# Gate layer of a graph network: TensorE gathers three of sixteen tiles, GpSimd thirteen

## The chip, the cores and the metric

The kernel runs on one core of one Trainium2 chip. The metric is the device time of one execution in microseconds (us); shorter is better. The engines are TensorE (PE, with its weight loads PEld), VectorE (DVE), ScalarE (ACT), GpSimd (POOL) and SyncE (SP). They run side by side and wait for one another through semaphores.

## The reference, cut to what matters

Four graph layers run over 3,125 nodes with 96 features and 100,000 edges sorted by target node: a power iteration, three graph convolutions, a message layer and a gate layer. Each gets `relu(layernorm(x))` and is added to `x`. The change is in the gate layer (two small loads for it lie in the message layer):

```python
edge_input = concatenate([x[src], edge_attr], axis=-1)        # 96 + 32 features
messages = gelu(edge_input @ mW1 + mb1) @ mW2 + mb2
gates = sigmoid(gelu(edge_input @ gW1 + gb1) @ gW2 + gb2)
aggregated = segment_sum(messages * gates, dst)
combined = concatenate([x, aggregated], axis=-1)
h = x + gelu(combined @ uW1 + ub1) @ uW2 + ub2                # then a layernorm
```

## The kernel before, in words

The edges are cut into 784 tiles of 128 and these into 98 groups of 8 (`GT`). Two groups, an even and an odd one, make a pair. Each tile needs its 128 source nodes' values, and there are two ways to get them.

*By GpSimd.* At the end of the message layer the product of every node with both first weights (192 values) is written to a table in memory. For six tiles of each group (`BY`) GpSimd issues an indirect DMA that fetches 128 rows of that table into `rows`, a ring of seven groups (L1322). TensorE multiplies the tiles' edge features with the edge part of the weights (`mix_edges`, L1539): three tiles at a time lie in three blocks of 32 partitions, two halves make six products. VectorE adds the six products to the six gathered tiles with one instruction (`add_edges`, L1437).

*By TensorE.* For the other two tiles of each group (`ON`), thus four a pair or 512 edges, SyncE loads the source numbers to 125 partitions (`load_row`), ScalarE turns them into 16-bit numbers (`widen`, L1343), and VectorE compares them with each of 25 blocks of 125 node numbers (`make_picks`, L1412): 25 instructions a pair of 512 columns, 13 in one group and 12 in the next. TensorE multiplies these selection matrices with the nodes' features in two 16-bit parts (`collect`, L1549): 50 matmuls a pair into a PSUM bank, two banks taking turns. ScalarE copies the result to `inputs` (L1350), and TensorE applies bias and weights (`mix_inputs`, L1559 and L1562).

Then, for all eight tiles: ScalarE takes the gelu of both (`activate`, L1357 to L1365), into `gated` and into `passed`, which has six slots; VectorE forms the gate sum (`sum_gates`, L1443, L1446); ScalarE takes a tanh (L1371); VectorE makes one-hot target matrices (`make_onehots`, L1471, L1473, and the addition of earlier sums, L1454); TensorE sums the messages (`sum_messages`, L1573).

The order is written out by hand in turns. In turn t VectorE does the addition of group t, the gate sum of t-1, the one-hots of t-2 and half of the picks of a later pair:

```python
for turn in range(NG + 2):
    if turn < NG:
        add_edges(turn)
    if 0 < turn <= NG:
        sum_gates(turn - 1)
    if turn > 1:
        steps = make_onehots(turn - 2)
    if (turn + 4) // 2 < NG // 2:
        make_picks((turn + 4) // 2, turn % 2)
```

TensorE's turn is the edge products of the next group (these wait for VectorE's addition, as they share the banks), half a collection, the input products of the next group, and the message sums of t-2. GpSimd runs ahead until the ring of seven is full, then it waits for ScalarE's last read of a slot (`rows_used`). After its last gather it does two wide sums of 125 x 2400 elements (L1327, L1329), for the end of the layer.

Of the kernel before, what the change touches and what calls it, by code (L numbers as in the profile page):

```python
# [6 lines left out]
D = 96  # L7
# [17 lines left out]
EPS = 1e-5  # L25
LOADS = 23
FAR = 8192.0
# [5 lines left out]
EDGES = 4  # L33
ON = 2
BY = GT - ON
CUT = 13
ROW_LIFT = 4096.0
MIDDLE = 1600.0
KEPT = 6
SLOTS = 3  # L40
# [761 lines left out]


def tiles_picked(groups):

    return groups // 2 * PICKED + groups % 2 * 2


class GateInputs:


    def __init__(self, nc, ctx, weights):
# [11 lines left out]
        self.t = space[0:NP, 6272:6272 + NT * D].rearrange("p (t d) -> p t d", d=D)  # L824
        self.gate_pick = space[0:NP, 8704:8704 + NT * ON * EP].bitcast(F16).rearrange("p (t e) -> p t e", t=NT)
        self.parts = m.sb("parts", [NP, NT, 2 * D], F16)
# [3 lines left out]
        self.wh = m.sb("wh", [D, 2 * D], F32)  # L830
        self.we = m.sb("we", [3 * DE, 2 * D], F32)
        self.b1 = m.sb("b1", [NP, 2 * D], F32)
# [24 lines left out]
def message_layer(nc, g, src_rows, dst, edges, w1, b1, w2, b2, pre):  # L857

    with ExitStack() as ctx:
# [40 lines left out]
        def _(sp):  # L900
# [12 lines left out]
            for group in range(NG):  # L913
# [307 lines left out]
def gated_layer(nc, g, pre, edges_T, on_edges_T, on_src, out):  # L1221
# [4 lines left out]
    with ExitStack() as ctx:  # L1226
# [13 lines left out]
        src_row = m.sb("src_row", [NP, 2, 2 * ON * EP], I32)  # L1240
        src_near = m.sb("src_near", [NP, 2, 2 * ON * EP], F16)
        ones = m.sb("ones", [128, 128], BF16)
        bias = m.sb("bias", [128, ON, 2 * D], BF16)
        bias_part = m.sb("bias_part", [NP, 2, 2 * D], BF16)
# [30 lines left out]
        def _(sp):  # L1275
# [3 lines left out]
            def load_row(c):  # L1279
                if c >= 2:  # L1280
                    sp.wait_ge(widened, c - 1)
                sp.dma_start(src_row[:, c % 2, :], on_src[c, :].unsqueeze(0).to_broadcast([NP, 2 * ON * EP])
                             ).then_inc(row_loaded[c % 2], 16)
# [26 lines left out]
        def _(pool):  # L1310
# [22 lines left out]
        def _(act):  # L1333
# [12 lines left out]
            def collect(c):  # L1346
                act.wait_ge(gathered, 2 * (c + 1))
                if c >= 2:
                    act.wait_ge(on_mixed, 2 * (c - 1))
                nc.scalar.activation(inputs[0:D, c % 2, :], collected[c % 2], ACT.Copy).then_inc(collected_out, 1)  # L1350

            def activate(group):
                r = rows[:, group % RING, :, :]
# [3 lines left out]
                nc.scalar.activation(gated[:, group % 2, BY:GT, :], product[:, :, D:2 * D], ACT.Gelu  # L1357
                                     ).then_inc(gate_in, 1)
                if group >= KEPT:
                    act.wait_ge(group_done, group - KEPT + LAG + 1)  # L1360
                nc.scalar.activation(passed[:, group % KEPT, BY:GT, 0:D], product[:, :, 0:D], ACT.Gelu
                                     ).then_inc(on_used, 1)
                act.wait_ge(added, group + 1)
                nc.scalar.activation(gated[:, group % 2, 0:BY, :], r[:, :, D:2 * D], ACT.Gelu).then_inc(gate_in, 1)
                nc.scalar.activation(passed[:, group % KEPT, 0:BY, 0:D], r[:, :, 0:D], ACT.Gelu  # L1365
                                     ).then_inc(rows_used, 1)
# [31 lines left out]
        def _(dve):  # L1398
# [25 lines left out]
            link(nc.vector.tensor_tensor(bias_rest[:, 1, :], bias_rest[:, 0, :], bias_part[:, 1, :], ALU.subtract))  # L1424
            for k in range(ON):
                link(nc.vector.tensor_copy(bias[0:1, k, :], b1[0:1, :]))
# [97 lines left out]
        def _(pe):  # L1524
# [7 lines left out]
            def mix_edges(group):  # L1532
                pe.wait_ge(edge_ready[group % SLOTS], 16 * (group // SLOTS + 1))
                if group:
                    pe.wait_ge(added, group)
                for half in range(2):
                    for k in range(3):
                        at = slice(DE * k, DE * (k + 1))
# [4 lines left out]
            def collect(c, part):  # L1543
                pe.wait_ge(picked, NT * c + (CUT, NT)[part])
                if c >= 2:
                    pe.wait_ge(collected_out, c - 1)
                for j in range(*((0, CUT), (CUT, NT))[part]):
                    for i in range(2):
                        last = nc.tensor.matmul(collected[c % 2], parts[:, j, i * D:(i + 1) * D], pick[:, j, :],  # L1549
                                                start=(j == 0 and i == 0), stop=(j == NT - 1 and i == 1))  # L1550
                last.then_inc(gathered, 1)

            def mix_inputs(group):
# [3 lines left out]
                if group:  # L1557
                    pe.wait_ge(on_used, group)
                nc.tensor.matmul(product, ones[:, :], bias[:, :, :], start=True, stop=False)  # L1559
                for i in range(ON):  # L1560
                    at = (group % 2 * ON + i) * EP
                    last = nc.tensor.matmul(product[:, i, :], inputs[:, c % 2, at:at + EP], w1[:, :],  # L1562
                                            start=False, stop=(i == ON - 1))
                last.then_inc(on_mixed, 1)
# [136 lines left out]
```

## Time and profile before

| | us |
|---|---|
| median of three runs | 3346.31 (3342.11 to 3347.23) |
| the profiled execution | 3346.54 |
| its span | 3344.5 |
| granted TensorE clock over the span | 0.948 |
| busy: PE / DVE / POOL / ACT | 2896.9 / 2424.0 / 1144.0 / 780.9 |

The gate layer takes about the last 970 us of the span. The numbers are of one profiled execution. In a line of a group, "x" is the count; then come busy time in us and the mean of one in ns, and the idle time of its engine just before, with what ended it. In a timeline a row is start, length, engine, line, operation, output<-input, shapes and count; instructions of one kind that follow each other are merged. Records of neighbouring VectorE instructions overlap by some 0.08 us. In a row of busy times by stretch come the stretch, its length, then PE, PEld, DVE, ACT and POOL with their counts, the granted TensorE clock, the share of the DMA engines and GB/s.

### The profile page before, as it was taken

How to read it: one execution, taken by the hardware profiler on the slowest of the kernel's cores; microseconds unless marked ns; L12 is line 12 of the kernel's file. 1: busy time of each engine (PE TensorE's matmuls, PEld its weight loads, DVE VectorE, ACT ScalarE, POOL GpSimd, SP SyncE). 2: the span in 40 equal slices, each digit the busy share in tenths (PEclk: the TensorE clock that was granted, in tenths of full speed). 3: DMA queues.
4: the chain of work that ended last, by engine and by line, in shares of the span. 5: the costliest groups of instructions: out<-in, count | busy, mean ns of one | idle time of the engine just before them, and what ended most of it. 6: DMA issues, size and time to landing. Idle time of an engine off the chain costs nothing. (4 is left out here: it accounts for less than half of the span.)

```text
span 3344.5 us, 73809 instructions
## 1 busy us (share of the span) xinstructions
PE 2896.9 (87%) x25677; PEld 2247.1 (67%) x25678; DVE 2424.0 (72%) x6174; ACT 780.9 (23%) x1414; POOL 1144.0 (34%) x1156
## 2 busy tenths in 40 slices
PE   3677777899999988899799999998699999999985
PEld 0211211699999987777799999997466666666654
DVE  6988777743333364335888888886699999999996
ACT  0133455610000014110211111111133333333321
POOL 0000000000000000000777777774477666666650
PEclk9999989889999998999899999998699999999997
DMA  0000000000000000000544454441344333333320
GB/s 29 0 0 0 0 0 0 2 2 2 2 2 2 2 2 4 1 1 13 134 122 113 117 119 120 118 116 40 90 106 104 98 94 96 98 94 96 98 63 15
DMA packets 102571, 176.68 MB, mean 53 GB/s; under 512 B 35467, under 2 KB 57408, under 8 KB 102284
## 3 DMA queue, kind: packets, MB, share of 16 engines
q0 software_dynamic: 45472, 84.37, 11.1%
q1 hardware_dynamic: 56811, 88.29, 9.3%
q8 instruction: 204, 3.34, 0.4%
q14 instruction: 84, 0.68, 0.1%
HBM read 167.77 MB, written 4.80 MB: 52 GB/s over the span
## 5 line engine op out<-in xcount | busy, mean ns | idle before, releaser
L1322 POOL DMA_INDIRECT gate_rows<-first_rows,all_src_i x588 | 586.2, 997 | 264.3 <-issue 157.3
L951 POOL DMA_INDIRECT msg_rows<-h_rows,all_src_i x539 | 535.7, 994 | 164.2 <-issue 163.8
L1147 PE MATMUL msg_sums<-pre_parts,pre_space 125*128 125x192 f16 x6125 | 528.6, 248 | 37.3 <-DVE pre_space L1025 37.2
L1549 PE MATMUL gate_sums<-pre_space,pre_parts 125*96 125x512 f16 x2450 | 552.3, 382 | 7.0 <-DVE pre_parts L1418 7.0
L938 POOL MEMSET pre_middle<- 125x1 f32 x1 | 0.1, 99 | 1590.6 <-POOLq L649 1590.6
L1147 PEld LDWEIGHTS msg_sums<-pre_parts,pre_space 125*128 125x128 f16 x6125 | 510.3, 99 | 44.0 <-DVE pre_space L1025 39.1
L579 PE MATMUL hop_sums<-dense_work,dense_counts 125*128 125x192 f16 x6250 | 520.6, 247 | 14.2 <-DVE dense_t L533 6.6
L579 PEld LDWEIGHTS hop_sums<-dense_work,dense_counts 125*128 125x128 f16 x6250 | 518.1, 98 | 16.6 <-DVE dense_t L533 7.2
L1549 PEld LDWEIGHTS gate_sums<-pre_space,pre_parts 125*96 125x96 f16 x2450 | 295.1, 124 | 241.0 <-issue 33.0
L422 PE MATMUL cnt_sums<-cnt_hot,cnt_near 128*128 x1000 | 346.2, 407 | 120.2 <-DVE cnt_hot L361 115.0
L1025 DVE TENSOR_SCALAR pre_space<-msg_src_near,pre_node_no 125x640 f16<-125x640 f16 x1225 | 393.7, 394 | 12.0 <-ACT msg_src_near L963 11.8
L1412 DVE TENSOR_SCALAR pre_space<-gate_src_near,pre_node_no 125x512 f16<-125x512 f16 x1225 | 375.1, 379 | 15.4 <-PE gate_sums L1549 8.3
L422 PEld LDWEIGHTS cnt_sums<-cnt_hot,cnt_near 128*128 x1000 | 97.3, 97 | 363.0 <-issue 360.2
L533 DVE TENSOR_REDUCE dense_t<-hop_sums 125x384 f32<-125x768 f32 (+1 forms) x63 | 54.9, 871 | 291.5 <-PE hop_sums L579 291.5
L359 DVE TENSOR_TENSOR cnt_near<-dense_work,cnt_src_n 128x256 f16 x500 | 180.1, 360 | 111.6 <-issue 87.2
L785 PE MATMUL conv_sums<-dense_work,dense_counts 125*128 125x288 bf16 x1875 | 235.7, 290 | 7.9 <-DVE dense_t L714 7.9
L239 ACT ACTIVATE dense_work<-cnt_key,cnt_start_at 128x786 f32<-128x786 f32 x158 | 150.2, 951 | 387.2 <-PE cnt_sums L422 341.0
L785 PEld LDWEIGHTS conv_sums<-dense_work,dense_counts 125*128 125x128 f16 x1875 | 185.8, 99 | 57.6 <-DVE dense_t L714 8.6
L979 ACT ACTIVATE msg_rows<-msg_rows 128x768 f32<-128x768 f32 x98 | 82.7, 844 | 580.5 <-DVE msg_rows L1052 580.5
L367 DVE TENSOR_SCALAR cnt_hot<-dense_work 128x500 f16 x500 | 173.8, 348 | 0.0
L361 DVE TENSOR_SCALAR cnt_hot<-dense_work 128x500 f16 x500 | 172.2, 344 | 0.0
L1573 PE MATMUL gate_sums<-gate_onehot,gate_passed 128*97 128x64 f32 x1584 | 155.9, 254 | 15.4 <-DVE gate_onehot L1473 15.4
(261 smaller groups left out, 3268.4 us busy)
## 6 DMA issues: line engine op xcount, KB each, us to landing
msg_edge<-edges SPq DMA_DIRECT2D x98, 384.0 KB
msg_src_row<-src_rows SPq DMA_DIRECT2D x49, 312.5 KB
gate_src_row<-on_src SPq DMA_DIRECT2D x49, 250.0 KB
gate_edge<-edges SPq DMA_DIRECT2D x98, 96.0 KB
gate_rows<-first_rows,all_src_i POOLq DMA_INDIRECT x588
msg_rows<-h_rows,all_src_i POOLq DMA_INDIRECT x539
gate_inputs<-on_edges SPq DMA_DIRECT2D x49, 64.0 KB, 1.8
first_rows<-pre_space SPq DMA_DIRECT2D x6, 375.0 KB
```

The lines of the kernel that those rows point to most:

```text
L359: nc.vector.tensor_tensor(nears.rearrange("p (c i) -> p c i", i=2), pairs2, low, ALU.is_equal)
L361: nc.vector.tensor_scalar(hots[0], iota, codes[:, 0:ET][:, bass.ds(now, 1)], None, ALU.is_equal).then_inc(ready[0], 1)
L367: nc.vector.tensor_scalar(hots[1], iota, code, None, ALU.is_equal).then_inc(ready[1], 1)
L422: end_of_pair = nc.tensor.matmul(sums[:, b, 0:WIN * NT], nears.rearrange("p (c i) -> p i c", i=2)[:, i, :], hots[i], start=False, stop=Tru ...
L579: last = nc.tensor.matmul(sums[:, g0 + i, 0:2 * D], counts[0:NP, at:at + 128], half[frm][:, k, :], start=(k == 0), stop=(k == NT - 1))
L785: last = nc.tensor.matmul(sums[:, 4 * (q % 2) + i, 0:3 * D], counts[0:NP, at:at + 128], parts[:, j, :], start=(j == 0), stop=(j == NT - 1))
L951: nc.gpsimd.indirect_dma_start(out=rows[:, r, k, :], out_offset=None, in_=table, in_offset=bass.IndirectOffsetOnAxis(ap=src_i[:, at:at + 1 ...
L1025: nc.vector.tensor_scalar(pick[:, c % 2, j, :], src_near[:, c % 2, :], node_no[:, j:j + 1], 1.0 / ROW_LIFT, ALU.is_equal, ALU.mult).then_i ...
L1147: last = nc.tensor.matmul(got[group % 2][:, n, 0:2 * D], pick[:, c % 2, j, i * EP:(i + 1) * EP], parts[:, j, :], start=(j == 0), stop=(j = ...
L1322: nc.gpsimd.indirect_dma_start(out=rows[:, r, k, :], out_offset=None, in_=table, in_offset=bass.IndirectOffsetOnAxis(ap=src_i[:, at:at + 1 ...
L1412: nc.vector.tensor_scalar(pick[:, j, :], src_near[:, c % 2, :], node_no[:, j:j + 1], 1.0 / ROW_LIFT, ALU.is_equal, ALU.mult).then_inc(pick ...
L1549: last = nc.tensor.matmul(collected[c % 2], parts[:, j, i * D:(i + 1) * D], pick[:, j, :], start=(j == 0 and i == 0), stop=(j == NT - 1 an ...
```

## The change

TensorE gathers one tile of each even group and two of each odd one (`ON = (1, 2)`), so 384 edges a pair (`PAIR`) for 512; GpSimd gathers seven and six. The picks, the collected values, the source numbers and the inputs shrink to 384 columns. The seventh tile's edge features lie in a fourth block of 32 partitions, in a half of four tiles; `we` gets a fourth copy of the weights (two more loads in the message layer, `LOADS`). The fourth block's products take PSUM bank 3, so the sums move to 4 and 5, and the collection has bank 6 alone instead of two in turn: TensorE waits for ScalarE's copy before it collects anew. The addition becomes two instructions, one for each half. `passed` has five slots for six.

```diff
-ON = 2
-BY = GT - ON
+ON = (1, 2)
+PAIR = sum(ON) * EP
-KEPT = 6
+KEPT = 5
+def by_dma(group):
+    return GT - ON[group % 2]
...
-        rows = m.sb("rows", [EP, RING, BY, 2 * D], F32)
+        rows = m.sb("rows", [EP, RING, GT - 1, 2 * D], F32)
-        edge = m.sb("edge", [3 * DE, SLOTS, 2, EP], F32)
-        inputs = m.sb("inputs", [D + DE, 2, 2 * ON * EP], F32)
+        edge = m.sb("edge", [4 * DE, SLOTS, 2, EP], F32)
+        inputs = m.sb("inputs", [D + DE, 2, PAIR], F32)
-        total = [sums[0:D + 1, b, 0:SPAN] for b in (3, 4)]
-        collected = [sums[0:D, b, :] for b in (5, 6)]
-        product = sums[:, 7, 0:ON * 2 * D].rearrange("p (k d) -> p k d", k=ON)
+        total = [sums[0:D + 1, b, 0:SPAN] for b in (4, 5)]
+        collected = sums[0:D, 6, 0:PAIR]
+        product = [sums[:, 7, 0:n * 2 * D].rearrange("p (k d) -> p k d", k=n) for n in ON]
...
-                for k in range(BY):
+                for k in range(by_dma(group)):
                     at = group * GT + k
                     nc.gpsimd.indirect_dma_start(
...
             def add_edges(group):
-                turn, r = divmod(group, RING)
-                dve.wait_ge(rows_ready[r], 16 * BY * (turn + 1))
+                r, n = group % RING, by_dma(group)
+                dve.wait_ge(rows_ready[r], 16 * sum(by_dma(i) for i in range(r, group + 1, RING)))
                 dve.wait_ge(edge_mixed, group + 1)
-                to = rows[:, r, :, :].rearrange("p (h k) d -> p h k d", h=2)
-                products = sums[:, 0:3, 0:4 * D].rearrange("p k (h d) -> p h k d", h=2)
-                nc.vector.tensor_tensor(to, to, products, ALU.add).then_inc(added, 1)
+                for half, k0, k1 in ((0, 0, n - 3), (1, n - 3, n)):
+                    to = rows[:, r, k0:k1, :]
+                    products = sums[:, 0:k1 - k0, 2 * D * half:2 * D * (half + 1)]
+                    nc.vector.tensor_tensor(to, to, products, ALU.add).then_inc(added, 1)
...
             def mix_edges(group):
                 pe.wait_ge(edge_ready[group % SLOTS], 16 * (group // SLOTS + 1))
                 if group:
-                    pe.wait_ge(added, group)
-                for half in range(2):
-                    for k in range(3):
+                    pe.wait_ge(added, 2 * group)
+                for half, n in enumerate((by_dma(group) - 3, 3)):
+                    for k in range(n):
...
             def collect(c, part):
                 pe.wait_ge(picked, NT * c + (CUT, NT)[part])
-                if c >= 2:
-                    pe.wait_ge(collected_out, c - 1)
+                if c:
+                    pe.wait_ge(collected_out, c)
...
-                nc.tensor.matmul(product, ones[:, :], bias[:, :, :], start=True, stop=False)
-                for i in range(ON):
-                    at = (group % 2 * ON + i) * EP
+                n, to = ON[group % 2], product[group % 2]
+                nc.tensor.matmul(to, ones[:, :], bias[:, 0:n, :], start=True, stop=False)
+                for i in range(n):
+                    at = (group % 2 * ON[0] + i) * EP
```

## Rows read from the trace of the kernel before

**Rows 1.** Busy time by engine, steady part of the gate layer (first: window length).

```profile
2605.00:3214.00 609.00, 583.14 (x3946) 402.38 (x3946) 572.65 (x1260) 188.37 (x408) 406.95 (x408) 1.00 0.37 96
```

**Rows 2.** Waits in the layer: who waited for whom, us in total, times, longest.

```profile
POOL gate_rows L1322 <- ACT gate_passed L1365: 102.5, 71, 1.7
PE gate_sums L1539 <- DVE gate_rows L1437: 35.5, 44, 1.6
DVE gate_rows L1437 <- PE gate_sums L1539: 2.4, 1, 2.4
```

**Rows 3.** Timeline, VectorE's additions: start us, us, engine line, operation.

```profile
2423.93 1.34 DVE L1437 TENSOR_TENSOR gate_rows<-gate_rows,gate_sums 128x1152 f32<-128x1152 f32 x1
...
2506.03 1.33 DVE L1437 TENSOR_TENSOR gate_rows<-gate_rows,gate_sums 128x1152 f32<-128x1152 f32 x1
...
2524.22 1.33 DVE L1437 TENSOR_TENSOR gate_rows<-gate_rows,gate_sums 128x1152 f32<-128x1152 f32 x1
...
3214.52 1.34 DVE L1437 TENSOR_TENSOR gate_rows<-gate_rows,gate_sums 128x1152 f32<-128x1152 f32 x1
```

**Rows 4.** Timeline, VectorE's picks in stretches, two beside gathers, one without.

```profile
2511.26 3.71 DVE L1412 TENSOR_SCALAR pre_space<-gate_src_near,pre_node_no 125x512 f16<-125x512 f16 x12
...
2520.13 4.17 DVE L1412 TENSOR_SCALAR pre_space<-gate_src_near,pre_node_no 125x512 f16<-125x512 f16 x13
...
3239.26 3.23 DVE L1412 TENSOR_SCALAR pre_space<-gate_src_near,pre_node_no 125x512 f16<-125x512 f16 x12
```

**Rows 5.** Timeline, single gathers and picks, message layer first.

```profile
2165.72 0.95 POOL L951 DMA_INDIRECT msg_rows<-h_rows,all_src_i  x1 [0.30 <-issue]
2166.06 0.37 DVE L1025 TENSOR_SCALAR pre_space<-msg_src_near,pre_node_no 125x640 f16<-125x640 f16 x1
2166.36 0.45 DVE L1025 TENSOR_SCALAR pre_space<-msg_src_near,pre_node_no 125x640 f16<-125x640 f16 x1
...
2511.87 0.95 POOL L1322 DMA_INDIRECT gate_rows<-first_rows,all_src_i  x1 [0.30 <-issue]
2512.12 0.34 DVE L1412 TENSOR_SCALAR pre_space<-gate_src_near,pre_node_no 125x512 f16<-125x512 f16 x1
2512.38 0.55 DVE L1412 TENSOR_SCALAR pre_space<-gate_src_near,pre_node_no 125x512 f16<-125x512 f16 x1
```

**Rows 6.** Groups by line, VectorE: count, busy us, mean ns, idle before.

```profile
L1045 DVE TENSOR_TENSOR msg_rows<-msg_sums,msg_edge 128x192 f32<-128x192 f32 x49 | 16.7, 341 | 2.5 <-PE msg_sums L1147 2.5
```

**Rows 7.** GpSimd: first gather (timeline), gathers of 2424 to 2587.6 by line.

```profile
2378.91 0.95 POOL L1322 DMA_INDIRECT gate_rows<-first_rows,all_src_i  x1 [4.51 <-DMA first_rows<-pre_space]
...
L1322 POOL DMA_INDIRECT gate_rows<-first_rows,all_src_i x127 | 126.2, 994 | 38.7 <-issue 38.7
```

**Rows 8.** Timeline, TensorE's collections and ScalarE's copy of one.

```profile
2167.39 6.35 PE L1147 MATMUL msg_sums<-pre_parts,pre_space 125*128 125x192 f16 x75
...
2392.20 13.87 PE L1549 MATMUL gate_sums<-pre_space,pre_parts 125*96 125x512 f16 x50 [6.97 <-DVE pre_parts L1418]
...
2720.83 0.59 ACT L1350 ACTIVATE gate_inputs<-gate_sums 96x512 f32<-96x512 f32 x1 [4.26 <-PE gate_sums L1549]
...
2724.57 5.81 PE L1549 MATMUL gate_sums<-pre_space,pre_parts 125*96 125x512 f16 x26
```

**Rows 9.** Busy time by engine, part of the counting stage (columns as before).

```profile
500.00:700.00 200.00, 161.72 (x2124) 98.86 (x2124) 152.31 (x446) 110.24 (x192) 0.00 (x0) 0.84 0.00 1
```

**Rows 10.** Timeline, the first 25 picks of message layer and gate layer.

```profile
1603.53 7.97 DVE L1025 TENSOR_SCALAR pre_space<-msg_src_near,pre_node_no 125x640 f16<-125x640 f16 x25 [2.22 <-ACT msg_src_near L963]
...
2381.66 7.87 DVE L1412 TENSOR_SCALAR pre_space<-gate_src_near,pre_node_no 125x512 f16<-125x512 f16 x25 [7.03 <-ACT gate_src_near L1343]
```

**Rows 11.** Timeline around GpSimd's wide sums, and VectorE's last addition.

```profile
3224.95 5.28 POOL L1327 TENSOR_TENSOR pre_space<-all_h,pre_ub 125x2400 f32<-125x2400 f32 x1
3224.97 11.29 DVE L1443 TENSOR_TENSOR pre_space<-pre_space,pre_gw 128x768 f32<-128x768 f32 x1
...
3277.56 1.35 DVE L1437 TENSOR_TENSOR gate_rows<-gate_rows,gate_sums 128x1152 f32<-128x1152 f32 x1
```

More of the change, by code:

```diff
@@ L25 @@
 EPS = 1e-5
-LOADS = 23
+LOADS = 25
 FAR = 8192.0
@@ L925, in _ @@
                         sp.dma_start(to, frm).then_inc(pre.loaded, 16)
-                    for k in range(3):
+                    for k in range(4):
                         sp.dma_start(pre.we[DE * k:DE * (k + 1), 0:D],
@@ L1349, in collect @@
                     act.wait_ge(on_mixed, 2 * (c - 1))
-                nc.scalar.activation(inputs[0:D, c % 2, :], collected[c % 2], ACT.Copy).then_inc(collected_out, 1)
+                nc.scalar.activation(inputs[0:D, c % 2, :], collected, ACT.Copy).then_inc(collected_out, 1)
             def activate(group):
-                r = rows[:, group % RING, :, :]
+                n, values = by_dma(group), product[group % 2]
+                r = rows[:, group % RING, 0:n, :]
                 act.wait_ge(on_mixed, group + 1)
@@ L1356, in activate @@
                     act.wait_ge(gate_sum, group - 1)
-                nc.scalar.activation(gated[:, group % 2, BY:GT, :], product[:, :, D:2 * D], ACT.Gelu
+                nc.scalar.activation(gated[:, group % 2, n:GT, :], values[:, :, D:2 * D], ACT.Gelu
                                      ).then_inc(gate_in, 1)
@@ L1424, in _ @@
             link(nc.vector.tensor_tensor(bias_rest[:, 1, :], bias_rest[:, 0, :], bias_part[:, 1, :], ALU.subtract))
-            for k in range(ON):
+            for k in range(2):
                 link(nc.vector.tensor_copy(bias[0:1, k, :], b1[0:1, :]))
@@ L1534, in mix_edges @@
                 if group:
-                    pe.wait_ge(added, group)
-                for half in range(2):
-                    for k in range(3):
+                    pe.wait_ge(added, 2 * group)
+                for half, n in enumerate((by_dma(group) - 3, 3)):
+                    for k in range(n):
                         at = slice(DE * k, DE * (k + 1))
@@ L1544, in collect @@
                 pe.wait_ge(picked, NT * c + (CUT, NT)[part])
-                if c >= 2:
-                    pe.wait_ge(collected_out, c - 1)
+                if c:
+                    pe.wait_ge(collected_out, c)
                 for j in range(*((0, CUT), (CUT, NT))[part]):
                     for i in range(2):
-                        last = nc.tensor.matmul(collected[c % 2], parts[:, j, i * D:(i + 1) * D], pick[:, j, :],
+                        last = nc.tensor.matmul(collected, parts[:, j, i * D:(i + 1) * D], pick[:, j, :],
                                                 start=(j == 0 and i == 0), stop=(j == NT - 1 and i == 1))
@@ L1558, in mix_inputs @@
                     pe.wait_ge(on_used, group)
-                nc.tensor.matmul(product, ones[:, :], bias[:, :, :], start=True, stop=False)
-                for i in range(ON):
-                    at = (group % 2 * ON + i) * EP
-                    last = nc.tensor.matmul(product[:, i, :], inputs[:, c % 2, at:at + EP], w1[:, :],
-                                            start=False, stop=(i == ON - 1))
+                n, to = ON[group % 2], product[group % 2]
+                nc.tensor.matmul(to, ones[:, :], bias[:, 0:n, :], start=True, stop=False)
+                for i in range(n):
+                    at = (group % 2 * ON[0] + i) * EP
+                    last = nc.tensor.matmul(to[:, i, :], inputs[:, c % 2, at:at + EP], w1[:, :],
+                                            start=False, stop=(i == n - 1))
                 last.then_inc(on_mixed, 1)
@@ L1669 @@
     src, dst = padded(inputs["src"], 0), padded(inputs["dst"], N)
+    blocks = [[[0, 1, 2, 3], [4, 5, 6, 7]], [[0, 1, 2, 6], [3, 4, 5, 7]]]
     edges_32 = padded(inputs["edge_attr_32"], 0).reshape(NG, GT, EP, DE)
@@ L1676 @@
                                    axis=1).reshape(NG // 2, PICKED * EP),
-        "on_src": src.reshape(NG, GT, EP)[:, BY:].reshape(NG // 2, 2 * ON * EP),
+        "on_src": np.concatenate([src.reshape(NG, GT, EP)[i::2, GT - ON[i]:] for i in range(2)],
+                                 axis=1).reshape(NG // 2, PAIR),
         "dst": np.ascontiguousarray(dst.reshape(ET, EP).T),
@@ L1682 @@
                                          .transpose(0, 2, 1, 3)).reshape(NG, EP, GT * D),
-        "edges_32": np.ascontiguousarray(edges_32[:, 0:BY].reshape(NG, 2, 3, EP, DE)
-                                         .transpose(0, 2, 4, 1, 3)).reshape(NG, 3 * DE, 2 * EP),
-        "on_edges_32": np.ascontiguousarray(edges_32[:, BY:].reshape(NG // 2, 2, ON, EP, DE)
-                                            .transpose(0, 4, 1, 2, 3)).reshape(NG // 2, DE, 2 * ON * EP),
+        "edges_32": np.ascontiguousarray(np.stack([edges_32[i::2, blocks[i]] for i in range(2)], axis=1)
+                                         .transpose(0, 1, 3, 5, 2, 4)).reshape(NG, 4 * DE, 2 * EP),
+        "on_edges_32": np.ascontiguousarray(np.concatenate([edges_32[i::2, GT - ON[i]:] for i in range(2)], axis=1)
+                                            .transpose(0, 3, 1, 2)).reshape(NG // 2, DE, PAIR),
     }
```

20 lines of the change are left out of this document (10 added, 10 removed).

## Prediction

> **What bounds the kernel now.** I read the page first: the profiled execution took 3346.54 us, of which its span is 3344.5, against a median of 3346.31, so a difference worked out in the span is taken off 3346.5 as it stands. Then the busy table of the steady part of the gate layer: in 609 us VectorE is busy for 572.65 and TensorE for 583.14, GpSimd for 406.95, ScalarE for 188.37 [rows 1]. Two engines at 94 to 96% could each be the bound, so the list of waits decides. TensorE waits 44 times, 35.5 us in all, for VectorE's addition of the edge products; GpSimd waits 102.5 us for ScalarE to free a row slot; and VectorE waits for that same product of TensorE once in 98 groups, 2.4 us [rows 2]. VectorE is the bound. The reader is to see that TensorE's high share is not the limit, and that GpSimd is ahead.
>
> The yardstick is the start of VectorE's addition L1437: two groups (a pair) take 2524.22 - 2506.03 = 18.19 us while GpSimd still runs freely, and the 44 pairs from 2423.93 to 3214.52 take 790.6 us, 17.97 each on average, since once the ring of seven slots is full GpSimd pauses [rows 3].
>
> VectorE's largest item is the picks L1412, 25 a pair. Where no gather runs, twelve take 3.23 us; beside gathers twelve take 3.71 and thirteen 4.17 [rows 4]. As the record of one pick overlaps the next by about 0.08, the undisturbed step is (3.23 - 0.34) / 11 = 0.263 us. The single picks show where the rest goes: the one that starts 0.25 us after a gather's start takes 0.34, the next, at +0.51, takes 0.55. In the message layer the pick at +0.34 is undisturbed (0.37) and the one at +0.64 takes 0.45 [rows 5]. So near its end a gather holds a pick up. Where it lets go is 2512.38 + 0.55 - 0.08 - 2511.87 = 0.98 us after the gather's start. Gathers come every 1.25 us. Today's picks start at 0.98, 1.24, 0.25 and 0.51 of this cycle and the fourth is held: four picks per gather.
>
> **The change, part by part.** *Picks.* Their width falls from 512 to 384. From 640 to 512 columns the undisturbed pick goes from 0.37 to 0.34 [rows 5], so 128 columns are worth 0.03 by the two digits of these rows; I take 0.033, which lies within their rounding, and the step becomes 0.230. But the time beside gathers is set by the cycle. Starting at 0.98, picks of 0.230 start at 1.21, then 0.19, 0.42 and 0.65 of the next cycle; the last would end at 0.88 and is held to 0.98. That is five per gather, with 0.10 lost where 0.21 was. Today's stretches by the same rule: the first pick (0.64 after the gather of 2510.62) is held for 0.34, then twelve picks take 0.34 + 2 x 1.25 + 3 x 0.263 = 3.63 and thirteen 0.34 + 3 x 1.25 = 4.09, which are the 3.71 and 4.17 of [rows 4] less the overlap. After: 0.34 + 2 x 1.25 + 0.23 = 3.07 and 3.30. A pair of stretches falls from 7.72 to 6.37: -1.35 us. Bounds: nothing gained beside gathers (first rival), or no holding at all, 25 x 0.230 = 5.75. I take 6.37, which only extends what reproduces today's two stretches.
>
> The Trainium skill (page "SBUF — State Buffer", section "Who interferes with whom") says that VectorE in such a mode and GpSimd take one pair of ports, and that whoever issues first has it for the whole instruction while the other is blocked. The trace agrees that they exclude each other but not with the length: if a gather held the pair for its 0.95 us, 25 picks would need 5.75 + 5 x 0.95 = 10.5 us, and 7.7 are measured. Its clause on who issues first is the third rival below.
>
> *Addition of edge products.* One instruction of 1152 elements becomes two: 768 + 576 in even groups, 576 + 576 in odd ones. From 192 elements in 341 ns [rows 6] and 1152 in 1337 the slope is 1.04 ns per element: 0.94 us for 768 and 0.74 for 576, as steps 0.86 and 0.66 against 1.26 now. A pair goes from 2.52 to 1.52 + 1.32 = 2.84: +0.32 us. This is on the path in full.
>
> *GpSimd.* Thirteen gathers a pair for twelve. In the free stretch 127 gathers take 126.2 + 38.7 = 164.9 us, 1.298 each [rows 7]: 13 make 16.88 us.
>
> *VectorE's pair* becomes 18.19 + 0.32 - 1.35 = 17.16 us, 0.28 above GpSimd's 16.88. GpSimd starts some 29 us ahead (its gathers begin at 2378.91 [rows 7], so those of group 2 at about 2378.9 + 15.7 = 2394.6, and VectorE adds to group 2 at 2423.93), stays ahead and hardly pauses. So the relief that VectorE has today from GpSimd's pauses (18.19 against 17.97 on average) goes, which is why I count from 18.19. Over 44 pairs: 44 x (17.97 - 17.16) = -35.6 us.
>
> *TensorE.* A collecting matmul of 512 columns has a step of 5.81 / 26 = 0.223 us, one of 192 columns 6.35 / 75 = 0.085 [rows 8]; by their slope 384 columns take 0.168. 50 a pair give -2.8 us, and even groups lose one input product. Of 17.97 us a pair it is busy today for 583.14 / 609 = 96%, 17.2; that becomes some 14, with over 3 us idle: worth nothing on the path. The seventh tile in the fourth row block adds two of fourteen records to 0.93 us of small matmuls, and even as two serial ones (0.3) it lies in that idle time. If TensorE idles more its clock may dip: in the counting stage, busy 161.72 of 200 us, the granted clock was 0.84 against 1.00 here [rows 1, 9]. At 0.84 its 14 us a pair would be 16.7: still hidden.
>
> *One collecting bank for two.* The next collection waits for ScalarE's copy. The copy starts at 2720.83 and takes 0.59; the next collection starts at 2724.57 [rows 8]. 3.1 us of cover, made of input products, message sums and edge products, which stay. Zero; if the cover went it would cost up to 0.6 on TensorE, not on VectorE.
>
> *SyncE.* Edge blocks grow to 128 partitions, the index rows and inputs shrink by a quarter; they are asked for groups ahead. Two more small loads lie in the message layer. Five instead of six slots of `passed`: the one that is wanted is freed a turn before ScalarE writes it. Zero each.
>
> *Opening,* 2381.66 to 2423.93. Here TensorE's first collection (13.87 us for 50, at a low clock at first) [rows 8] and the first picks (7.87) [rows 10] are in series: -2.7 or so and -1.5, and the first pairs' picks and collections -1.8: together -6.
>
> *Tail,* from 3214.52 to 3277.56, 63.0 us. After the last gather GpSimd's two wide sums run 10.5 us, and L1443 on VectorE takes 11.29 instead of 0.94 [rows 11]. The sums now start at about 2378.9 + 49 x 16.88 + 2 = 3208, when VectorE is near group 95: the 10.3 us are paid as before. After: 2 pairs of 17.16, 3 turns without picks of 5.4, and 10.3: 60.8. -2.2 us.
>
> Sum: -35.6 - 6 - 2.2 = -43.8. 3346.5 - 43.8 = 3302.7, say 3302.5 us.
>
> **Rivals.** *First, slower: still four picks per gather.* For it: 25 picks of 640 columns took 7.97 us beside gathers and 25 of 512 took 7.87 [rows 10]: narrowing brought next to nothing once, since both are four per 1.25. It decides at one point: the pick that starts 0.42 after the gather's start and ends at 0.65. If it is held, the picks gain nothing, the addition's 0.32 stays, and a pair takes 18.51. Against: the message layer's pick from 0.34 to 0.64 is not held [rows 5], practically the same stretch. Price: 44 x 0.54 = +23.8, opening -4, tail +1: 3367 us. Chance 0.12.
>
> *Second, only the columns.* The holds cost what they cost today in total (their phase shifts, and one gather more per pair makes up for a shorter hold), and the picks give 25 x 0.033 = 0.83. A pair 17.68: 44 x 0.29 = -12.8, opening -5, tail -1: 3328 us. For it: holds depend on phases which I only know for today's lengths. Chance 0.20.
>
> *Third, gathers wait for picks, and GpSimd becomes the bound.* Five gathers a pair would each wait up to one pick, 0.23: 16.88 + 1.15 = 18.03, 49 pairs from 2378.9 end at 3262. The last addition then comes at about 3265 instead of 3277.6, but GpSimd's wide sums hold VectorE for 10.3 after it: 3344 us, no change. The skill's clause that issue order decides who blocks would do this. Against: gathers beside picks last 0.95 like others [rows 5]. Chance 0.07.
>
> *Fourth, no holding at all:* VectorE 16.54, so GpSimd's 16.88 is the bound: 44 x 1.09 = -48 and -8: 3290 us. Chance 0.06. My forecast: 0.55.
>
> **Numbers.** 0.2% of 3346 us, 6.7 us, is about what a measurement of this kernel can tell from no change. The range runs from the fourth case to a little beyond the second, 3289 to 3335, and leaves out the first and third (0.19). Faster: forecast, second and fourth, and a little of the third: 0.83; the same 0.05; slower 0.12.
>
> **What would show it.** Right: L1412's successor with 384 columns, twelve in about 3.1 us and thirteen in 3.4 beside gathers; two additions a group; additions 17.1 to 17.2 us apart per pair; few GpSimd waits for ScalarE; TensorE at some 80%. Wrong: most gathers with only four picks between two holds, additions over 18 us apart per pair, gathers of 1.1 us or more beside picks, or VectorE waiting for gathered rows.

## The result, and the profile after

The changed kernel takes 3302.35 us (median of four runs, 3298.76 to 3305.37) against 3346.14 before: ratio 0.9871, 95% interval 0.9859 to 0.9883, so 43.8 us or 1.3% faster. The profiled execution took 3305.37 us with a span of 3303.6; against 3346.54 and 3344.5 before that is -41. The median falls on the forecast to a fraction of a microsecond. That is luck: the four runs lie 6.6 us apart, and of the steps behind the forecast some were off and cancelled.

The busy times of two steady stretches (length, PE, PEld, DVE, ACT, POOL, granted clock, DMA share, GB/s), for [rows 1]:

```profile
2415.00:2585.00 170.00, 150.41 (x1160) 119.19 (x1159) 158.88 (x392) 52.63 (x121) 131.16 (x128) 0.95 0.39 106
2600.00:3165.00 565.00, 500.47 (x3803) 395.59 (x3802) 519.62 (x1279) 173.00 (x396) 435.31 (x426) 0.93 0.39 105
```

TensorE is down from 96% to 88.6% busy (500.47 of 565 us), VectorE from 94 to 92%, and GpSimd up from 67 to 77% (435.31 of 565). The granted clock is 0.93 to 0.95, where it was 1.00. The waits, for [rows 2]:

```profile
POOL gate_rows L1327 <- issue: 193.8, 636, 0.3
...
PE gate_sums L1546 <- DVE gate_rows L1444: 93.0, 65, 2.4
DVE gate_rows L1444 <- DMA gate_rows<-first_rows,all_src_i: 18.8, 24, 3.4
```

GpSimd's wait for ScalarE is gone from the list: between its 637 gathers there are only the 0.3 us from one to the next, so it runs without a pause. A new wait is there: VectorE's addition waits for gathered rows, 24 times, 18.8 us. VectorE's additions, start and length, for [rows 3] (groups 2, 22, 36 and 90), then the two additions of a group by shape:

```profile
2415.09 0.94 DVE L1444 TENSOR_TENSOR gate_rows<-gate_rows,gate_sums 128x768 f32<-128x768 f32 x1
...
2584.26 0.94 DVE L1444 TENSOR_TENSOR gate_rows<-gate_rows,gate_sums 128x768 f32<-128x768 f32 x1
...
2702.97 0.95 DVE L1444 TENSOR_TENSOR gate_rows<-gate_rows,gate_sums 128x768 f32<-128x768 f32 x1 [0.34 <-DMA gate_rows<-first_rows,all_src_i]
...
3169.23 0.94 DVE L1444 TENSOR_TENSOR gate_rows<-gate_rows,gate_sums 128x768 f32<-128x768 f32 x1
```

```profile
L1444 DVE TENSOR_TENSOR gate_rows<-gate_rows,gate_sums 128x576 f32<-128x576 f32 x133 | 95.5, 745 | 4.0 <-DMA gate_rows<-first_rows,all_src_i 4.0
L1444 DVE TENSOR_TENSOR gate_rows<-gate_rows,gate_sums 128x768 f32<-128x768 f32 x45 | 42.6, 946 | 4.5 <-DMA gate_rows<-first_rows,all_src_i 4.4
```

44 pairs take 3169.23 - 2415.09 = 754.1 us, 17.14 each: -36.4 us. But the first ten take 16.92 each and the other 34 17.20, as if something slower had taken over. The border lies at group 36, the first whose addition waits for its rows: the 17 pairs up to it take 16.93 each, the 27 behind it 17.27. GpSimd's gathers by line, for [rows 7], early and late:

```profile
L1327 POOL DMA_INDIRECT gate_rows<-first_rows,all_src_i x128 | 131.9, 1030 | 39.0 <-issue 39.0
...
L1327 POOL DMA_INDIRECT gate_rows<-first_rows,all_src_i x431 | 441.3, 1024 | 131.3 <-issue 131.3
```

A gather now takes (131.9 + 39.0) / 128 = 1.335 us and later 1.329, against 1.298: 13 of them 17.3 us. That is more than VectorE's 16.9, so GpSimd's lead shrinks and its gathers then set the pace. The lead, from the end of a group's last gather to its addition, is 9.3 us at group 2 (20.9 in the kernel before), 5.0 at group 22, 1.7 at group 36, and stays near 2. VectorE's 24 waits for rows lie accordingly: none before 2702.97, then 6 up to 2800, 4 up to 3000, 8 up to 3170, and 6 in the tail. The last gather ends at 3227.30 and the last addition starts at 3229.59. So the end of the layer is set by when GpSimd starts and by its 637 gathers; how fast VectorE was in the first pairs only used up the lead. The picks in stretches and single ones, for [rows 4, 5] (in the single ones each gather stands with some of the picks beside it):

```profile
2471.15 3.20 DVE L1418 TENSOR_SCALAR pre_space<-gate_src_near,pre_node_no 125x384 f16<-125x384 f16 x13
2474.27 1.41 DVE L1444 TENSOR_TENSOR gate_rows<-gate_rows,gate_sums 128x576 f32<-128x576 f32 x2
...
2479.61 3.20 DVE L1418 TENSOR_SCALAR pre_space<-gate_src_near,pre_node_no 125x384 f16<-125x384 f16 x12
```

```profile
2471.67 0.31 DVE L1418 TENSOR_SCALAR pre_space<-gate_src_near,pre_node_no 125x384 f16<-125x384 f16 x1
2471.75 1.04 POOL L1327 DMA_INDIRECT gate_rows<-first_rows,all_src_i  x1 [0.30 <-issue]
2472.36 0.31 DVE L1418 TENSOR_SCALAR pre_space<-gate_src_near,pre_node_no 125x384 f16<-125x384 f16 x1
...
2480.06 0.52 DVE L1418 TENSOR_SCALAR pre_space<-gate_src_near,pre_node_no 125x384 f16<-125x384 f16 x1
2480.81 0.94 POOL L1327 DMA_INDIRECT gate_rows<-first_rows,all_src_i  x1 [0.30 <-issue]
2481.25 0.31 DVE L1418 TENSOR_SCALAR pre_space<-gate_src_near,pre_node_no 125x384 f16<-125x384 f16 x1
2481.48 0.36 DVE L1418 TENSOR_SCALAR pre_space<-gate_src_near,pre_node_no 125x384 f16<-125x384 f16 x1
```

Thirteen picks take 3.20 us (4.17 before); twelve take 3.20 in this stretch, since the one at 2480.06 is held to 0.52 (0.31 alone) beside a gather that took 1.16. In the second part of the rows of single ones the pick at 0.44 us after the gather's start runs through and the one at 0.67 is held by only 0.05: the five-pick rhythm. In the first part it is the other way round: the pick at 0.61 runs through and the gather takes 1.04 instead of 0.95. Of such gathers there were none among the rows of [rows 5].

What holds a gather up is the VectorE instruction that is under way when it starts. The pick of 2471.67 ends at 2471.98 and the gather of 2471.75 at 2472.79, 0.81 later by these digits, 0.82 by those of the trace. The same holds for VectorE's product with the gate weights:

```profile
2467.18 0.95 DVE L1450 TENSOR_TENSOR pre_space<-pre_space,pre_gw 128x768 f32<-128x768 f32 x1
2467.41 1.53 POOL L1327 DMA_INDIRECT gate_rows<-first_rows,all_src_i  x1 [0.30 <-issue]
```

Gathered over the whole layer, 235 gathers of the changed kernel took over 0.965 us, and 226 of them end 0.82 us (to 0.01) after such an instruction: 133 after a pick, 55 after the product, 37 after an instruction that makes one-hots, 1 after another. In the kernel before it was 92 of 92: 71 after one-hots, 18 after the product, 1 after a pick, 2 after others. No gather was held by an addition (L1437, L1444) or by the sum that follows the product (L1446, L1453), though 98 and 23 started beside one in the changed kernel.

The rhythm can be counted too. From one gather's start to the next, where only picks ran, the kernel before has four picks in 117 of 189 cases and five in 72. The changed kernel has the forecast five in 36 of 98 cases, with a gather of 0.95 us; in the other 62 six picks start and the gather takes 1.05.

The tail, for [rows 11]: additions of groups 95, 96 and 97, and GpSimd's wide sum:

```profile
3212.94 1.42 DVE L1444 TENSOR_TENSOR gate_rows<-gate_rows,gate_sums 128x576 f32<-128x576 f32 x2 [3.43 <-DMA gate_rows<-first_rows,all_src_i]
...
3221.48 1.62 DVE L1444 TENSOR_TENSOR gate_rows<-gate_rows,gate_sums 128x768 f32<-128x768 f32 x2 [3.15 <-DMA gate_rows<-first_rows,all_src_i]
...
3227.33 5.27 POOL L1332 TENSOR_TENSOR pre_space<-all_h,pre_ub 125x2400 f32<-125x2400 f32 x1
3229.59 1.42 DVE L1444 TENSOR_TENSOR gate_rows<-gate_rows,gate_sums 128x576 f32<-128x576 f32 x2 [2.51 <-DMA gate_rows<-first_rows,all_src_i]
3230.92 7.68 DVE L1450 TENSOR_TENSOR pre_space<-pre_space,pre_gw 128x768 f32<-128x768 f32 x1
```

Each addition comes after a wait of 2.5 to 3.4 us for rows. The last one is 3229.59 - 3169.23 = 60.4 us after that of group 90 (63.0 before), although no wide sum lies between. It now comes after: L1450 takes 7.68 us instead of 0.95, and from the last addition to the span's end there are 74.0 us instead of 66.9. The opening, for [rows 10, 8]:

```profile
2380.96 5.91 DVE L1418 TENSOR_SCALAR pre_space<-gate_src_near,pre_node_no 125x384 f16<-125x384 f16 x25 [6.80 <-ACT gate_src_near L1348]
...
2389.54 10.94 PE L1556 MATMUL gate_sums<-pre_space,pre_parts 125*96 125x384 f16 x50 [5.32 <-DVE pre_parts L1424]
```

### The profile page after: what moved, and what is told of

Read it like the earlier page. It is cut to its first block, busy times and chain, and to the rows that moved or that the text cites. A ratio compares the mean times of both kernels' runs of the same rounds, so it can differ in the third digit from the quotient of the medians.

```text
span 3303.6 us, 73960 instructions
## 1 busy us (share of the span) xinstructions
PE 2807.4 (85%) x25677; PEld 2263.3 (69%) x25678; DVE 2368.9 (72%) x6272; ACT 768.1 (23%) x1414; POOL 1212.1 (37%) x1205
## 4 chain that ended last, share of the span: by engine, by line
POOL 32%; issue 10%; DVE 5%; PE 2%; DMA 1%; DVEq 0%; ACT 0%; POOLq 0%; ACTq 0%
POOL gate_rows L1327 20%; POOL msg_rows L956 13%; DVE pre_space L1030 2%; PE msg_sums L1152 1%; PE msg_sums L1167 0%; DMA first_rows<-pre_space 0%; DVE msg_rows L1054 0%; DVE pre_space L1450 0%; DMA msg_rows<-h_rows,all_src_i 0%; PE gate_sums L1581 0%; ACT msg_src_near L968 0%; DMA msg_src_row<-src_rows 0%; DVE pre_space L1122 0%; DVE msg_rows L1050 0%; DVE all_h L1518 0%
## 5 line engine op out<-in xcount | busy, mean ns | idle before, releaser
L1327 POOL DMA_INDIRECT gate_rows<-first_rows,all_src_i x637 | 655.1, 1028 | 198.3 <-issue 193.8
L1556 PE MATMUL gate_sums<-pre_space,pre_parts 125*96 125x384 f16 x2450 | 459.7, 349 | 5.3 <-DVE pre_parts L1424 5.3
L1556 PEld LDWEIGHTS gate_sums<-pre_space,pre_parts 125*96 125x96 f16 x2450 | 315.3, 132 | 140.5 <-issue 30.8
L1030 DVE TENSOR_SCALAR pre_space<-msg_src_near,pre_node_no 125x640 f16<-125x640 f16 x1225 | 393.6, 395 | 11.6 <-ACT msg_src_near L968 11.3
L1418 DVE TENSOR_SCALAR pre_space<-gate_src_near,pre_node_no 125x384 f16<-125x384 f16 x1225 | 302.3, 320 | 12.1 <-ACT gate_src_near L1348 6.8
L1546 PE MATMUL gate_sums<-pre_we,gate_edge 32*128 32x192 f32 x1274 | 101.6, 379 | 100.6 <-DVE gate_rows L1444 93.0
```

Of the source, the lines that this page charges most:

```text
L1030: nc.vector.tensor_scalar(pick[:, c % 2, j, :], src_near[:, c % 2, :], node_no[:, j:j + 1], 1.0 / ROW_LIFT, ALU.is_equal, ALU.mult).then_i ...
L1327: nc.gpsimd.indirect_dma_start(out=rows[:, r, k, :], out_offset=None, in_=table, in_offset=bass.IndirectOffsetOnAxis(ap=src_i[:, at:at + 1 ...
L1418: nc.vector.tensor_scalar(pick[:, j, :], src_near[:, c % 2, :], node_no[:, j:j + 1], 1.0 / ROW_LIFT, ALU.is_equal, ALU.mult).then_inc(pick ...
L1556: last = nc.tensor.matmul(collected, parts[:, j, i * D:(i + 1) * D], pick[:, j, :], start=(j == 0 and i == 0), stop=(j == NT - 1 and i == 1))
```

## The experiments

Ratios are to the kernel before, on the same chip, with 95% intervals. First the parts of the change alone.

**Only narrow picks and collections.**

```diff
-  tensor_scalar(pick[:, j, :], src_near[:, c % 2, :], ...)
+  tensor_scalar(pick[:, j, 0:384], src_near[:, c % 2, 0:384], ...)
-  matmul(collected[c % 2], parts[...], pick[:, j, :], ...)
+  matmul(collected[c % 2][:, 0:384], parts[...], pick[:, j, 0:384], ...)
```

> Kernel before, with only the narrowing: picks, collecting matmuls and ScalarE's copy work on 384 of the 512 columns; the fourth tile's values of a pair are left at zero (so one tile of sixteen is left out of the computation). GpSimd keeps 12 gathers a pair, the addition stays one instruction. Theory A (the rhythm of picks and gathers: five picks per gather instead of four): the picks of a pair fall from 7.7 to 6.3 us, additions 16.6 to 16.8 us apart per pair, 45 pairs give -55 us, opening -6: 3285 us. Theory B (each pick saves only its columns, 0.033 us, and the time lost beside gathers stays as it is): 25 x 0.033 = 0.83 us a pair, -37 us and -5: 3304 us.

Measured: 3268.18 us, ratio 0.9763 (0.9747 to 0.9779), -79 us, 17 us more than theory A gave. Columns alone (B) would be 3304. Its gathers, 2430 to 3150 us:

```profile
L1323 POOL DMA_INDIRECT gate_rows<-first_rows,all_src_i x530 | 559.5, 1056 | 161.6 <-issue 161.6
```

They take 1.056 us each without the gap, 1.36 with it, and GpSimd no longer pauses though it has twelve a pair. Its pair is 12 x 1.36 = 16.3 us, just under VectorE's 16.44 (723.6 us for the 44 pairs from group 2), and no addition waits for rows. The mean is above the changed kernel's 1.03 because of the product and not of the picks: 87 gathers wait for the product (55 in the changed kernel), 135 for a pick (133).

**Only the thirteenth gather.** In even groups `indirect_dma_start` is issued once more, into a spare buffer.

> Kernel before, with only the gather added: in even groups GpSimd fetches a seventh tile into a buffer that nobody uses (passed has five slots to make room); the output is complete. Theory A: GpSimd needs 16.9 us a pair, VectorE 18.2, so VectorE stays the bound, but GpSimd no longer pauses and VectorE keeps its 18.19 us a pair to the end instead of 17.92: +10 us, 3356 us. Theory B (gathers cost VectorE nothing that depends on their number): 3346 us. If gathers themselves were the bound at 18.2 or more: 3360 or more.

Measured: 3352.41 us, 1.0013 (1.0003 to 1.0022), +4 to 5 us: VectorE stays the bound and loses a part of the relief from GpSimd's pauses, half of what A gave. A was wrong in that GpSimd no longer pauses: it still waits for ScalarE 21 times, 35.3 us in all, for 71 times and 102.5 us before.

**Only the split addition.**

```diff
-  to = rows[:, r, :, :] (both halves)
-  tensor_tensor(to, to, products, ALU.add)
+  for half in range(2):
+      tensor_tensor(rows[:, r, 3 * half:3 * half + 3, :], ..., sums[:, 0:3, 192 * half:192 * (half + 1)], ALU.add)
```

> Kernel before, with only the addition of the edge products split into two instructions of 576 elements, output complete. By the row durations the second instruction adds its fixed 0.06 us per group: 94 x 0.06 = +6 us, 3352 us. Rival (it also shifts the rhythm of picks and gathers, or lets ScalarE and TensorE start no earlier): anything beyond 3346 to 3356 us.

Measured: 3354.22 us, 1.0027 (1.0017 to 1.0036), +8.4 us, somewhat above the 6 expected, which the interval (6 to 12 us) still touches, and inside the band (3346 to 3356) beyond which the rival was to begin.

**Only the two restrictions.** `collected` twice bank 6, the wait on the last copy, `KEPT = 5`.

> Kernel before, with the two small restrictions of the change and nothing else: one collecting bank instead of two, five slots of passed instead of six, output complete. Theory: both lie in cover (ScalarE copies the bank 3 us before TensorE wants it): 3346 us, within 0.1%. Rival: TensorE, busy 96%, loses up to 0.6 us a pair: +28 us at most, 3374 us.

Measured: 3343.99 us, 0.9997 (0.9988 to 1.0007). Nothing, as forecast.

**The picks' width, in the changed kernel.** `src_near` and `pick` get 512 (448) columns, of which TensorE reads 384.

> Changed kernel, with picks as wide as before: 512 columns, of which the last 128 are compared with zeros and used by nobody; all else as changed, the output is complete. Theory A: four picks per gather again, a pair takes 18.19 + 0.32 = 18.5 us: 3361 to 3367 us, slower than before the change. Theory B: the picks give back 25 x 0.033 = 0.83 us a pair: 3302 + 38 = 3340 us.

> Changed kernel, with picks 448 columns wide (the last 64 compared with zeros, used by nobody), output complete. It looks for the point that decides between four and five picks per gather. A pick's step is 0.246 us, so after a hold ends at 0.98 us after a gather's start the picks start at 1.23, then 0.22 and 0.47 of the next cycle and, if the last of these runs through, 0.71. In the traces of before picks that start 0.42 us after a gather's start run through and those at 0.50 are held. Theory A: if 0.47 is held, four per gather as at 512 columns: 3358 to 3364 us. If it runs through, five: 3302 to 3310 us. Rival (columns alone): halfway between the 3302 of 384 and the 3363 of 512 columns, 3332 us.

Measured: 512 columns 3362.81 us, 1.0046 (1.003 to 1.0063); 448 columns 3307.8 us, 0.9887 (0.9871 to 0.9904); 384 columns 3302.35. The first 64 columns cost 5.5 us, the next 64 cost 55 (53 by the ratios). That is no slope in the kernel's time. But the first figure is small in part because at 384 columns gathers are the bound and hide VectorE's gain. VectorE's own pair, where no addition waits for rows, takes 16.93 us at 384 columns (groups 2 to 36), 17.33 at 448 and 18.49 at 512 (groups 2 to 90). By their steps alone 64 columns more are 25 x 0.016 = 0.41 us a pair. So the first 64 cost 0.40, about their columns, and the next 64 1.16: their columns and a step of 0.75. The picks from 2430 to 3150 us at 384, 448 and 512 columns (three kernels, in this order; count, busy time):

```profile
L1418 DVE TENSOR_SCALAR pre_space<-gate_src_near,pre_node_no 125x384 f16<-125x384 f16 x1050 | 259.8, 321 | 0.3
```

```profile
L1419 DVE TENSOR_SCALAR pre_space<-gate_src_near,pre_node_no 125x448 f16<-125x448 f16 x1041 | 276.6, 339 | 0.3
```

```profile
L1419 DVE TENSOR_SCALAR pre_space<-gate_src_near,pre_node_no 125x512 f16<-125x512 f16 x975 | 304.4, 385 | 0.3
```

Per pick 0.247, 0.266 and 0.312 us, over undisturbed steps of 0.230, 0.246 and 0.263. At 448 columns, a gather and two of its picks:

```profile
2794.43 0.95 POOL L1328 DMA_INDIRECT gate_rows<-first_rows,all_src_i  x1 [0.30 <-issue]
2794.90 0.33 DVE L1419 TENSOR_SCALAR pre_space<-gate_src_near,pre_node_no 125x448 f16<-125x448 f16 x1
2795.15 0.33 DVE L1419 TENSOR_SCALAR pre_space<-gate_src_near,pre_node_no 125x448 f16<-125x448 f16 x1
```

The pick 0.47 us after the gather's start and the one at 0.72 both run through. At 512 columns the one at 0.51 is held [rows 5]. The point that decides lies between. Counted from one gather's start to the next, where only picks ran, 96 of 102 cases at 448 columns have five picks, 164 of 189 at 512 have four.

Which of the two gives way goes with who was first. At 448 and 512 columns the pick under way at a gather's start had mostly begun 0.02 to 0.06 and 0.01 to 0.02 us before it, and in the whole layer 1 and 2 gathers waited for a pick. At 384 it had mostly begun 0.05 to 0.09 us before it, and 133 gathers waited (beside others the pick did).

**What bounds the changed kernel.** Three runs, and a fourth that bears on TensorE.

```diff
 # a_no_mult: VectorE's product left out
-  nc.vector.tensor_tensor(values, values, gw2_sb..., ALU.mult).then_inc(weighed, 1)
 # a_gather12: six gathers in even groups too
-  for k in range(by_dma(group)):
+  for k in range(6):
 # a_collect512: TensorE's matmuls at their old width
-  matmul(collected, parts[...], pick[:, j, :], ...)          # 384 columns
+  matmul(collected, parts[...], pick[:, j, :], ...)          # 512, the last 128 zeros
```

> Changed kernel, with VectorE's product with the gate weights (L1450) left out, so the gates are wrong: VectorE has 0.98 us less work per group. Theory A, second part (the trace after shows GpSimd's lead used up by the middle of the layer, so that GpSimd's 637 gathers are the bound from there): they still need 1.30 to 1.33 us each from 2378 us on and end at 3206 to 3226, so 0 to -25 us: 3277 to 3302 us, and VectorE waits much longer for gathered rows. Theory B, VectorE is the bound throughout: 96 x 0.98 = -94 us, 3210 us.

Measured: 3292.41 us, 0.984 (0.9824 to 0.9857). 94 us of VectorE's work went and 10 us came of it. VectorE's waits for rows in this kernel:

```profile
DVE gate_rows L1444 <- DMA gate_rows<-first_rows,all_src_i: 163.1, 90, 5.5
```

163.1 us instead of 18.8. The first ten pairs take 16.40 us and the rest 17.13, with some 2 us of lead left from group 7 on. So gathers are the bound there.

> Changed kernel, with the thirteenth gather of each pair left out: GpSimd fetches six tiles in even groups too, the seventh tile's rows stay at zero (so one tile of sixteen lacks its source values); the addition still covers seven. Theory A (GpSimd's gathers are the bound in the second half, and narrowing alone took 79 us of which the thirteenth gather and the split addition give back 34): a pair takes the 16.44 us of the narrowed kernel plus 0.32 for the split addition, 16.76 against 17.14 now: -17 us, 3285 us. If the split addition costs nothing: 3268 us. If VectorE is the bound and the gather is free: 3302 us.

Measured: 3285.94 us, 0.9819 (0.9802 to 0.9835), the total that theory A had. Here no addition waits for rows, and the pair takes 16.91 us (16.76 forecast), the same as the 16.93 of the changed kernel's first 17 pairs; there the later ones take 17.27. That is VectorE's pace without and with the gathers as the bound. The thirteenth gather costs the changed kernel 17 us, three times and more what it cost the kernel before.

> Changed kernel, with TensorE's collecting matmuls as wide as before: 512 columns, of which the last 128 are zeros that nobody uses; picks stay at 384, the output is complete. Theory A (TensorE's relief of 2.8 us a pair lies in its idle time): 3302 us, at most 3 more in the opening. Rival (TensorE at 17 us a pair plus its waits is as late as VectorE, and its relief was needed): a pair takes 17.4 or more, 3313 to 3325 us.

Measured: 3306.48 us, 0.9881 (0.9865 to 0.9898): +3 us by the ratios, which the two intervals (0.9865 to 0.9898 and 0.9859 to 0.9883) don't tell from nothing. TensorE's relief is worth nearly nothing in the changed kernel. It is not so with the gather's bound away:

> Kernel before, with only VectorE's picks narrowed to 384 of 512 columns (the fourth tile's are left at zero); TensorE collects 512 columns as before. The kernel with both narrowed took 3268 us. Theory A says of this one that TensorE, busy 17.2 us a pair, becomes the bound, so a pair takes 17.3 to 17.5 us: 3315 to 3320 us. Rival (TensorE's width never matters): 3268 to 3273 us.

Measured: 3301.5 us, 0.9863 (0.9846 to 0.9879), between the two expectations, 33 us above the kernel with both narrowed. TensorE there (2605 to 3150 us), and who waits for it over the whole run:

```profile
2605.00:3150.00 545.00, 545.00 (x3701) 376.29 (x3701) 497.48 (x1180) 161.54 (x382) 402.35 (x397) 1.00 0.38 103
...
DVE pre_space L1413 <- PE gate_sums L1550: 24.7, 44, 4.1
```

TensorE is busy for 545.00 of 545 us (ends of matmuls are modelled, so this says that it has no gap, not that it is at its peak). In this stretch VectorE waits for it 32 times, 12.3 us. So narrow picks alone make TensorE the bound at 17.0 to 17.1 us a pair, where both narrowed gave 16.44.

**The wide sums on VectorE.** Both `nc.gpsimd.tensor_tensor` behind the gathers become `nc.vector.tensor_tensor` at the layer's start.

> Changed kernel, with GpSimd's two wide sums (h plus a bias, x plus a shift) given to VectorE at the start of the layer, where it waits 7 us for the source numbers; the output is complete. Theory: in the changed kernel they still hold one product of VectorE for 10 us near the end, which goes, and their 2 x 2.7 us on VectorE lie in its first wait: -10 us, 3292 us. Rival: the first wait isn't free (the picks start later by 5 us, GpSimd's lead shrinks nothing), -5 us, 3297; or the hold was covered by other waits at the end: 3302.

> Kernel before, with GpSimd's two wide sums given to VectorE at the start of the layer. In the changed kernel this gave 4 us. Here the hold of 10.3 us on VectorE's product falls 50 us before the end, in a stretch where VectorE sets the pace: if it costs all of it, -10 us, 3336 us; if TensorE, which ran on during the hold, hides part of it, -3 to -6 us.

Measured: changed kernel 3298.0 us, 0.9856 (0.9839 to 0.9872), against 0.9871 without it, so about -5 us, of which the intervals leave none certain; kernel before 3335.22 us, 0.9969 (0.9956 to 0.9981), -10.6 us, the whole hold. In the changed kernel the hold was 6.7 us long (7.68 - 0.95) and lay behind the last addition.

## Why the prediction came out right, point by point

**VectorE is the bound before.** Right: narrowing VectorE's picks alone, with TensorE's matmuls as they were, takes some 45 us. TensorE was the next bound close behind: with its matmuls narrowed too it is 79 us.

**The picks' rhythm.** Right in the main point, that narrower picks leave the rhythm of four per gather: thirteen take 3.20 us where 3.38 was forecast with the overlap. The kernel with 512 columns lands at 3362.8, near the first rival's 3367 (its pair 18.49 for 18.51), and 448 columns at 3307.8, where five per gather is what the trace shows. The second rival (columns alone, 3328) falls with both. What I had wrong is who yields. I let picks wait for gathers only. That rhythm held in 36 of 98 cases; in 62 the gather waited and six picks ran. As gathers yield too, VectorE's pair was 16.93 us in the first 17 pairs and not 17.16 (at 448 columns, where a single gather waited for a pick, it is 17.33). One working in the prediction mixes two widths: the 10.5 us that it holds against 7.7 measured takes 5.75 us for 25 picks of 384 columns, but the 7.7 belongs to 512 columns, whose 25 steps are 6.6 us. The sum is then 11.3, and what it was to show, that a gather doesn't keep the picks out for its whole 0.95 us, stands.

**The addition.** Right: 745 and 946 ns as worked out (740 and 940); alone and for halves of three tiles +8.4 us.

**GpSimd.** This step failed. I took 1.298 us a gather, 16.88 a pair, and "stays ahead and hardly pauses". It never pauses, but because it is late: measured 1.33 and 17.3. Its lead was smaller as well. The 29 us ran from the first gather of group 2 to the addition in the kernel before; from the end of the last gather, in the changed kernel, it is 9.3. At some 0.4 us a pair (17.3 less 16.9) the 7.3 us above the final 2 last 18 pairs, and after 17 the first addition waits. From there on GpSimd set the pace, with waits of VectorE that I had named as a sign of being wrong.

The mechanism is in part the third rival's, gathers waiting for picks. Adding up what gathers took beyond 0.95 us between groups 2 and 90 gives 1.03 us a pair: 0.28 for picks, 0.24 for one-hots, 0.44 for the product, 0.08 unassigned. Before, in the stretch where GpSimd ran freely, it was 0.65, all for the product. So picks cost a quarter of the 1.15 that the rival gave; the rest is mostly that other gathers now fall beside the one-hots, which no run took apart.

So the pair that I put at 17.16 for VectorE is the mean of VectorE's 16.93 and GpSimd's 17.27. That 44 pairs gave -36.4 against -35.6 is luck: the two errors cancel.

**TensorE, the bank, SyncE.** Zero was right: 3 us or less, and 0.9997 for the bank and the slots. The granted clock was 0.93, above the 0.84 that I had allowed for, and TensorE stayed hidden. But the relief is free only because something else is the bound; without it narrow picks bring the kernel before 45 us and not 79.

**Opening.** -8.1 (34.1 us from the first pick to the addition of group 2, against 42.3) where -6 was given; it began 0.7 earlier too. The first collection took 10.94 us for 13.87, the first picks 5.91 for 7.87. With GpSimd as the bound this gain only shortened its lead.

**Tail.** This term was off by most: -2.2 forecast with the hold in it, +4.4 measured. The stretch to the last addition gave -2.7, by another way: the groups waited for rows (8 to 9 us each, 5.4 forecast), and the hold moved behind the last addition, where it adds 7.1 us. With -0.7 - 8.1 - 36.4 - 2.7 + 7.1 the profile's -41 are complete. The remaining 3 us to the -43.8 of the medians are the profiled run, the slowest of the four.

The parts add up by ratios: narrowing -2.37%, split addition with its seventh tile +0.56% (kernel with twelve gathers less the narrowed one; 19 us, where 44 x 0.32 = 14 was forecast), thirteenth gather +0.52% (17 us): -1.29%.

Not settled: why the picks of 384 columns fall so that more of them begin early enough before a gather to hold it. No run shifted their start alone. Nor was it tried to give some pairs the fourth tile back, which would balance VectorE's 16.9 with GpSimd's 17.3.

## What to carry to other kernels

Where two engines hold each other up in a fixed rhythm, the cost of an instruction can jump at a certain length (here 0.75 us a pair between 448 and 512 columns): lay its starts out over one period of the other engine before pricing a shorter one per column. When the bound engine is relieved, reprice the next one under the new rhythm, not by its old mean, and count its lead from the end of its work: 2.4% more per gather decided here which engine was the bound. And check a total that fits against the terms, since two errors may hide in it.

## What the runs showed of the hardware

- Picks of 384, 448 and 512 columns differ by 0.016 us each when alone, but the kernel takes 3302, 3308 and 3363 us.
- An indirect gather of 128 rows that nothing held took 0.95 us of GpSimd and 0.30 to the next. A gather that VectorE held ended 0.82 us after the VectorE instruction that was under way at its start, 92 of 92 times before and 226 of 235 after. Picks (fp16), the product of two SBUF operands and the one-hot instructions held gathers; additions with a PSUM operand and the gate's sum over 96 elements held none.
- The other way round, a pick of 512 columns that began 0.51 us after a gather's start was held until 0.98, and one of 448 columns that began at 0.47 ran through, both beside gathers of 0.95 us.
- Two wide sums on GpSimd held VectorE's product of 0.95 us to 11.29 before and 7.68 after. Moved to VectorE they gave back 10.6 us of the first.
- In the steady stretches TensorE was granted 1.00 of its clock before (583.14 of 609 us busy) and 0.93 in the changed kernel (500.47 of 565), where the clock was at its lower level of 1.2 GHz for 80.6 of the 565 us. In the kernel with only the narrowing it was 0.99 at 486.00 of 545 us busy, so the busy share alone doesn't tell the clock.
